# Half of every layer 0 tile loaded by ScalarE's DMA queue, issued behind its copies of a panel

## The reference

```
u = par_u0*par_u1*(diag_u*x[:nu] @ W_u) + x[:nu];  i = the same for the items
e = concat(u, i)
h = adj @ (adj.T @ e)                      # layer 0
x = layernorm(x + layernorm(h)*gamma + beta + x)
T1 = adj @ x                               # layer 1, Chebyshev, K = 4
T2 = 2*(adj @ T1) - x;  T3 = 2*(adj @ T2) - T1
x = layernorm(x + x@w0 + T1@w1 + T2@w2 + T3@w3 + bias)
```

## Time and profile before

| | us |
|---|---|
| median of 3 runs | 1260.94 (1258.61 to 1261.74) |
| the profiled execution | 1265.37 |
| its span, first to last instruction | 1263.5 |
| PE busy | 1144.8 (91%) |
| DVE busy | 903.3 (71%) |
| ACT busy | 353.7 (28%) |
| SP's queue q1 | 247.84 MB, 72.5% of 16 engines' span |
| ScalarE's queue q10 | 110.11 MB, 30.5% |
| mean granted TensorE clock | 0.972 |

### The profile page before, as it was taken

The page is one execution under the profiler, slowest core; times in us unless marked ns, Lnnn a source line. Parts: engine busy times, 40 slices in busy tenths (PEclk is TensorE's granted clock), DMA queues, the critical chain, the costliest instruction groups (busy, mean ns, idle before and its releaser), DMA issues.

```text
span 1263.5 us, 14169 instructions
## 1 busy us (share of the span) xinstructions
PE 1144.8 (91%) x5155; PEld 503.7 (40%) x5164; DVE 903.3 (71%) x950; ACT 353.7 (28%) x634; POOL 62.4 (5%) x98
## 2 busy tenths in 40 slices
PE   4789999999999999889988999999899999589795
PEld 3335545545545544344423333433344444122221
DVE  2566876897888778679677776666576667678784
ACT  1445655655555556420100000000110000011111
POOL 0730000000000000010000000000000000011111
PEclk9979999999999999899999999999999999888998
DMA  7999999999999999979999999999999999999991
GB/s 230 253 288 247 285 294 277 283 278 287 289 285 283 281 279 268 213 145 316 264 296 346 346 328 314 293 303 263 282 283 338 315 317 320 341 310 345 351 352 49
DMA packets 393847, 361.28 MB, mean 286 GB/s; under 512 B 12252, under 2 KB 392452, under 8 KB 393812
## 3 DMA queue, kind: packets, MB, share of 16 engines
q1 hardware_dynamic: 280212, 247.84, 72.5%
q10 hardware_dynamic: 110880, 110.11, 30.5%
q0 software_dynamic: 2720, 2.86, 1.0%
HBM read 359.45 MB, written 1.31 MB: 286 GB/s over the span
## 4 chain that ended last, share of the span: by engine, by line
PE 44%; SPq 35%; DVE 8%; issue 4%; ACTq 4%; DMA 3%; ACT 1%; POOL 1%; DVEq 0%; POOLq 0%
PE bank L1118 29%; SPq L321 18%; SPq L332 16%; DVE turned L464 4%; PE bank L1169 4%; ACTq L274 4%; PE bank L1131 3%; DMA shared<-in_adj 3%; DVE xq L464 1%; PE bank L1147 1%; DVE shared L464 1%; PE bank L1274 1%; DMA raw<-in_adj 1%; PE bank L1084 1%; PE bank L1141 1%
## 5 line engine op out<-in xcount | busy, mean ns | idle before, releaser
L1118 PE MATMUL bank<-turned,terms 128*128 128x512 f32 x680 | 301.4, 596 | 5.0 <-DVE turned L464 3.3
L960 PE MATMUL bank<-shared 128*64 128x256 f32 x1600 | 231.3, 393 | 23.1 <-DMA shared<-in_adj 23.0
L484 DVE STREAM_TRANSPOSE shared<-shared 32x512 f32<-32x512 f32 x320 | 224.1, 700 | 4.1
L735 ACT COPY terms<-terms 32x512 f32<-32x512 f32 x320 | 197.1, 616 | 35.9 <-DVE terms L494 31.1
L464 DVE STREAM_TRANSPOSE turned<-shared 128x2048 f32<-128x2048 f32 x70 | 160.6, 2303 | 63.5 <-PE bank L1118 53.0
L464 DVE STREAM_TRANSPOSE turned<-raw 128x2048 f32<-128x2048 f32 x70 | 160.3, 2301 | 55.3 <-PE bank L1118 42.6
L1118 PEld LDWEIGHTS bank<-turned,terms 128*128 128x128 f32 x680 | 126.6, 190 | 170.9 <-issue 164.3
L960 PEld LDWEIGHTS bank<-shared 128*64 128x64 f32 x1600 | 115.4, 138 | 119.1 <-issue 55.1
L980 PE MATMUL bank<-scratch,t_cols 128*64 128x512 f32 x240 | 125.9, 606 | 10.9 <-ACT scratch L726 10.9
L1011 PE MATMUL bank<-turned,t_quart 128*64 128x512 f32 x160 | 83.9, 611 | 2.0 <-DVE t_quart L501 2.0
L972 PEld LDWEIGHTS bank<-ident,shared 128*128 128x128 f32 x480 | 52.1, 144 | 73.8 <-issue 66.0
(11 more groups left out here) (142 smaller groups left out, 1013.3 us busy)
## 6 DMA issues: line engine op xcount, KB each, us to landing
shared<-in_adj SPq DMA_DIRECT2D x100, 1024.0 KB, 11.4
raw<-in_adj SPq DMA_DIRECT2D x106, 512.0 KB, 10.1
raw<-in_adj ACTq DMA_DIRECT2D x106, 512.0 KB, 12.0
shared<-in_adj SPq DMA_DIRECT2D x104, 512.0 KB, 10.6
shared<-in_adj ACTq DMA_DIRECT2D x104, 512.0 KB, 12.0
raw<-in_adj SPq DMA_DIRECT2D x120, 256.0 KB, 7.9
xq<-in_x POOLq DMA_DIRECT2D x40, 32.0 KB, 6.9
out<-scratch POOLq DMA_DIRECT2D x40, 32.0 KB, 5.2
```

Of the source, the lines that this page charges most:

```text
L484: last = nc.vector.transpose(low_turned[Q32 * c:Q32 * (c + 1), :, :, Q32 * q:Q32 * (q + 1)], low[Q32 * q:Q32 * (q + 1), :, :, Q32 * c:Q32 ...
L735: last = nc.scalar.copy(spread[Q32 * c:Q32 * (c + 1), :, :, Q32 * q:Q32 * (q + 1)], across[Q32 * q:Q32 * (q + 1), :, c, :, :])
L960: last = nc.tensor.matmul(t_bank[H * odd:H * (odd + 1), 0:PW], e[:, s * SB + b, :], panels[slot][:, s * SB + b, :], start=(k == 0 and b < ...
L1118: last = nc.tensor.matmul(sum_bank[parity][:, :], terms[:, c * GB + i, columns], turned[place][:, i * BANK:(i + 1) * BANK], start=(first a ...
```

## The change

SP loads quarters 0 and 1 of every layer 0 tile, ScalarE's queue quarters 3 and 2. The bytes, the runs, the buffers and the semaphores are the same. ScalarE issues its halves of the first three tiles ahead of panel 1, of tiles 0 and 1 of the later groups behind its last spread copies of an even panel (ahead of `keep_t`), and of tile 2 behind its first copy of an odd panel.

```diff
             def load_layer0_tile(k, last, column):

                 if last is not None:
                     sp.wait_ge(tile_turned, last + 1 + RAW)
-                for q in (0, 2, 1, 3):
+                for q in (0, 1):
                     sp.dma_start(raw[k][Q32 * q:Q32 * (q + 1), :].rearrange("p (b c) -> p b c", c=P),
...
-            def layer0_panel(slot, j):
+            def load_upper(k, last, column):
+
+                if last is not None:
+                    act.wait_ge(tile_turned, last + 1 + RAW)
+                for q in (3, 2):
+                    act.dma_start(raw[k][Q32 * q:Q32 * (q + 1), :].rearrange("p (b c) -> p b c", c=P),
+                                  tile_rows[2 * SEGS[k] + 1][:, :, bass.ds(column + P * q, P)])\
+                        .then_inc(raw_loaded[k], DMA)
+
+            def layer0_panel(slot, j, two=None):

                 for i in range(ITEMS):
                     copy_turned(i, (j - 1) * ITEMS)
+                    if two is not None and slot == 1 and i == 0:
+                        load_upper(2, (two - 1) * TILED + 2, two * BANK)
                     spread_across(i, j)
+                if two is not None and slot == 0:
+                    for k in range(2):
+                        load_upper(k, (two - 1) * TILED + k, two * BANK)
                 keep_t(slot, j)
...
+            for k in range(TILED):
+                load_upper(k, None, 0)
             layer0_panel(1, 1)
             with act.Fori(1, NJ // 2) as two:
-                layer0_panel(0, two * 2)
-                layer0_panel(1, two * 2 + 1)
+                layer0_panel(0, two * 2, two)
+                layer0_panel(1, two * 2 + 1, two)
```

More of the change, by code:

```diff
@@ L275, in load_part @@
                             rows_of[:, :, at_column:at_column + SPAN * P]).then_inc(pair_loaded[u % SLOTS], DMA)
+        tile_rows = adj.rearrange("(g b i) c -> g i b c", b=BANK // Q32, i=Q32)
         def by_chunk(a, width):
@@ L312, in _ @@
             seg_rows = adj.rearrange("(s b p) c -> s p b c", p=P, b=SB)
-            tile_rows = adj.rearrange("(g b i) c -> g i b c", b=BANK // Q32, i=Q32)
             def load_layer0_tile(k, last, column):
```

## The result

In the first comparison, of 6 runs each, the changed kernel took a median of 1251.99 us (1250.12 to 1271.19) and the kernel before 1264.32 us (1258.61 to 1270.63); the ratio is 0.988, 95% interval 0.984 to 0.993. The ratio leaves out two of the changed kernel's six executions, 1271.1 and 1271.2 us, as slow ones, though their granted clock (0.974) is that of the others (0.973 to 0.975). The forecast was 1247, with 1241 to 1266 as its range. The profiled execution took 1253.07 us, its span 1251.3 against 1263.5. The profile of an execution in which the pairs gained nothing stands under "Once late".

What follows compares the result with a forecast made beforehand. Layer 0 was taken as DMA-bound by a small margin over TensorE's pace. 15 us gained in the pairs, 1 lost to ScalarE's issues and 0 at the start made 14 off the 1260.94 median: 1247 us, range 1241 to 1266.

Steps and rivals of the forecast that it cites:

- Bound: Layer 0, panels 4 to 19: DMA-bound by a small margin, late loads costing TensorE 15.8 us.
- my 371.9: Panels 4 to 19: us needed at TensorE's and ScalarE's own pace of 46.49 a pair, against 387.71 measured before.
- Gain in the pairs: Layer 0 panel pairs: TensorE stops waiting for segments, at most 15.8 us saved, 15 taken.
- Partition groups: Layer 0 tile loads: one group of 32 partitions gets about 200 GB/s, two groups at once the full rate.
- rival "no effect": Layer 0 loads: same engines and descriptors, the DMA pair stays at 48.46 us, total 1261; chance 0.13.
- 45.3 us a pair: Layer 0 loads after the change: 48.46 less 3.1 us, half the tile bytes moving at 348 instead of 206 GB/s.
- Even panel's end: ScalarE before L742: four DMAs take 2.4 us under 3.89 us of idle time, cost 0.
- The rival with dearer addresses: ScalarE's issues at 1.1 to 1.3 us each eat 5 to 12 us over 9 pairs: 1252 to 1259; chance 0.17.
- The "slower" rival: ScalarE's queue fills, issues last 1.83 us each, 31 us lost over 9 pairs: 1277; chance 0.15.
- Start: Panel 1: six DMAs make ScalarE 5 to 6 us late; between 4 us gained and 3 lost, 0 taken.
- the 2.13 us of the earlier trace: ScalarE's time for four such DMAs issued into an empty queue before the change, used to cost its new issues.

Runs made afterwards that it cites:

- Once late: Changed kernel repeated word for word: 1254.98 us, ratio 0.992; and with SP held once before its loads of panel 8: 1264.82 us, ratio 0.998.
- the left-out quarters: Changed kernel with quarters 2 and 3 of layer 0 tiles loaded by no queue (zeros): 1240.87 us, ratio 0.979 to the kernel before.
- the grouped version on one queue: Kernel before, SP alone issuing, tiles 0 and 1 together behind the odd panel's fourth segment, tile 2 behind the even's: 1248.68 us, ratio 0.987.
- both comparisons: Changed kernel against the kernel before, first 1251.99 us, ratio 0.988; then word for word again on another chip, 1254.98 us, ratio 0.992.
- the second profile: Profile of an execution of the changed kernel, repeated word for word: this execution 1258.86 us, the repeat's median 1254.98 us, ratio 0.992.
- a third moved: Changed kernel with only tile 2 of each group shared with ScalarE's queue, SP loading all of tiles 0 and 1: 1263.62 us, ratio 1.001.
- the two other starts: Changed kernel with ScalarE's first six DMAs behind panel 1's copies: 1272.33 us; or GpSimd's xq operations held until VectorE's second turn_across: 1272.51 us, ratio 1.003.
- eight, three and two places on one queue: Kernel before, SP alone: quarters spread over eight places a pair, 1294.99 us, ratio 1.020; unchanged, three; grouped in two, 1248.68 us, ratio 0.987.
- both placement tests: Changed kernel with the even panel's four DMAs behind the copies of t: 1267.28 us, ratio 1.004; with all quarters on ScalarE: 1325.51 us, ratio 1.046.

## Why the prediction was right, and where not

- **Bound.** Right. Late loads cost TensorE 15.8 us over panels 4 to 19; the left-out quarters and the grouped version on one queue reach the same 373.6 to 373.7 us, a little over my 371.9.
- **Gain in the pairs.** 15 forecast, 14.08 measured in the first profile and 0.34 in the second. The medians fell by 12.3 us in both comparisons against 14 forecast, but the executions differ: 10 of the 18 are below the quickest of before in their comparison, the other 8 are not. In the first profile the missing 1.7 us of 15.8 is panel 10: 26.09 us, where VectorE does its one-time work on the weights. Before, the wait for a segment hid it.
- **Partition groups.** Right for loads by themselves, and now shown apart from run length and queue: 205 GB/s for one group, 251 and 334 for groups 0 and 3 together. In the kernel it held in one profile (285) and not in the other (199 and 215). So the rival "no effect", pairs that stay at 48.46 us, is what the second profile shows with its 48.42, and the forecast is what the first shows.
- **45.3 us a pair.** This is the term that was mis-sized. It took 3.1 us off because half of the tile bytes would move at 348 GB/s. With runs of 512 bytes two groups at once got 251 by themselves and 285 in the first profile: by these rates the 1.57 MB take 6.3 and 5.5 us instead of 7.6, 1.3 to 2.1 us off, an estimate of 46.4 to 47.2 us a pair. That lies on both sides of the 46.49 that TensorE needs. Single profiles show 46.7 with SP ahead, and with SP late 48.4 for the change itself, 48.8 with a third moved, and 50.7 and 51.2 with the two other starts. The number of places where a queue goes between segments and quarters counts at least as much as the bytes: 53.96 (in a long execution), 48.46 and at most 46.7 us a pair for eight, three and two places on one queue. That the change helps in the median is shown; that it needs the second queue is refuted. That the forecast of 14 us came near the measured 12.3 is in part luck.
- **Even panel's end.** Right in both profiles (even panels of 24.4 us, but for panel 10): four DMAs under 3.89 us of cover, cost 0. The cover left was 3.47 us and not the 1 to 2 forecast, since they are issued beside the last spread copies. The rival with dearer addresses is out: 0.32 to 0.39 us each while there is room. The "slower" rival decides somewhere between four and eight DMAs, as both placement tests show.
- **Start.** The sum of 0 came out (0.96 us later), its parts did not. The fourth to sixth DMA held ScalarE for 14.3 us, most likely since the engines were full with SP's segments (SP issues without a pause from 10.94 us on): the 2.13 us of the earlier trace rows were taken in a queue with less beside it. Panel 1 gained 1.0 us, panel 2 lost 2.0, because VectorE's 16 copies began earlier beside GpSimd's second operation: 8.19 us against 5.84 before.
- **Not foreseen.** The scatter of the executions, 1248 to 1270 us in one comparison; the kernel before has one as wide (1256 to 1278). I expected a steady floor. That the loads' need is too near it fits the estimate above and the two profiles, and is not shown by a run of its own.

What stays open: why a queue loses time where it changes between segments and quarters. The busy share says that the transfers there are slower, and no more. Grouping also changes where the tiles stand among the segments, so "places" is the reading that fits three orders, not a mechanism. Nor is it shown why the two queues together move quarters at 277 to 293 GB/s with SP ahead and at 187 to 272 with SP late, which of the two brings about the other, and so why the shared version stays ahead in some executions only.

## What to carry to other kernels

Before moving loads to a second queue, look at the order on the first: try transfers into a few partitions together in one place, not in small lots between wide ones; here that gave 6 us more than the second queue, and steadily. If a second queue is used, here four short issues fit under 4 us of idle time and eight did not; count the issues against the room in the queue and the idle time in front of the next wait. A version that ends ahead by little is judged by the spread of its runs, not by one profile.

## What the hardware showed

- Loads into one group of 32 partitions moved 190 to 210 GB/s, whatever the run length (512 or 1024 bytes) and from one queue or two; groups 0 and 3 from two queues 251 (512 byte runs) or 334 (1024); over all partitions one queue moved 353 (1024 byte runs) or 304 (512).
- In the kernel two queues moved such quarters together at 277 to 293 GB/s in an execution with SP ahead, and at 196 to 272 and 187 to 228 in two with SP late (stretches of 2 us).
- Five further places a pair where one queue goes between wide and narrow transfers cost up to 5.5 us a pair, with the same bytes and a DMA share of 1.10 against 1.06.
- VectorE's 16 copies of 32 x 64 took 3.18 us alone and 8.19 us beside GpSimd's elementwise operation, ending 3.05 us after it; GpSimd's own times did not change (4.45 and 5.6 us), nor did its operations slow VectorE's 16 transposes in panel 2 (11.40 and 11.41 us).
- A DMA of 512 runs with a register address issued in 0.32 to 0.39 us on ScalarE while the queue had room. At the start, beside SP's segments, the fourth of six held the engine for 5.18 us and the fifth for 4.18.
